# Adding products that nobody reads to TensorE beside the norms and the solver parts of a three-block diffusion transformer

## What is computed

```python
for l in range(3):
    h = norm(x) * (1 + sc_msa) + sh_msa
    q, k, v = split(h @ w_qkv + b_qkv)        # layer 1 also norms q and k per head
    o = softmax(q @ k.T / 3) @ v              # 16 heads, 512 x 512 scores each
    x = x + g_msa * (o @ w_proj + b_proj)
    h = norm(x) * (1 + sc_mlp) + sh_mlp
    x = x + g_mlp * mlp(h)                    # layer 0: top 2 of 4 experts
U, _ = qr(P)                                  # P is 144 x 64
R = expm(skew(silu(cond) @ W.T + b))          # 64 x 64, one per sequence
z = x @ U
return x + (z @ R - z) @ U.T
```

## Time and profile before

| | us |
|---|---|
| runs of the kernel | 918.87 median (909.43, 918.87, 920.58) |
| the profiled execution | 919.2 |
| its span, first to last instruction | 917.2 |
| PE busy | 751.5 (82% of the span) |
| DVE busy | 556.0 (61%) |
| ACT busy | 386.0 (42%) |
| POOL busy | 181.0 (20%) |
| mean granted clock of PE | 0.856 |

### The profile page before, as it was taken

The page is one execution under the profiler, slowest core; times in us unless marked ns, Lnnn a source line. Parts: engine busy times, 40 slices in busy tenths (PEclk is TensorE's granted clock), DMA queues, the critical chain, the costliest instruction groups (busy, mean ns, idle before and its releaser), DMA issues.

```text
span 917.2 us, 11092 instructions
## 1 busy us (share of the span) xinstructions
PE 751.5 (82%) x3571; PEld 438.5 (48%) x3571; DVE 556.0 (61%) x1614; ACT 386.0 (42%) x690; POOL 181.0 (20%) x372
## 2 busy tenths in 40 slices
PE   6597889967998799798867886979897789979746
PEld 1353444335764445366444343645443555436325
DVE  3477787886327558752465777474787666785242
ACT  0221465534444544254235442435453356646511
POOL 5502012440132300302323003021003110021020
PEclk9955899989997669799977997976897988999957
DMA  3210100110121000012100000100000101000000
GB/s 88 69 35 7 32 14 22 39 31 13 48 56 32 1 24 13 12 33 60 39 18 1 24 12 13 32 1 1 24 13 11 33 1 25 12 12 1 13 1 13
DMA packets 22714, 21.23 MB, mean 23 GB/s; under 512 B 4831, under 2 KB 17015, under 8 KB 22658
## 3 DMA queue, kind: packets, MB, share of 16 engines
q1 hardware_dynamic: 22610, 20.52, 8.6%
q10 hardware_dynamic: 48, 0.02, 0.0%
HBM read 13.62 MB, written 0.61 MB: 16 GB/s over the span
## 4 chain that ended last, share of the span: by engine, by line
PE 62%; DVE 28%; issue 4%; ACT 2%; POOL 2%; DMA 0%; DVEq 0%; SPq 0%; ACTq 0%; POOLq 0%
PE m_bank L1400 11%; PE o_bank L1422 10%; DVE row_max L972 9%; PE s_bank L1383 8%; PE d_bank L1539 7%; PE d_bank L1483 3%; PE m_bank L1592 3%; PE m_bank L1409 2%; DVE h_tok L1031 2%; PE d_bank L1528 2%; PE d_bank L1440 2%; PE d_bank L1439 1%; PE d_bank L1454 1%; PE d_bank L1530 1%; PE d_bank L1529 1%
## 5 line engine op out<-in xcount | busy, mean ns | idle before, releaser
L797 ACT ACTIVATE probs<-s_bank 128x512 f32<-128x512 f32 x384 | 223.1, 598 | 380.4 <-PE s_bank L1383 377.1
L972 DVE TENSOR_REDUCE row_max<-m_bank 128x1 fp32r<-128x512 f32 x384 | 255.3, 686 | 91.8 <-PE m_bank L1400 86.5
L1400 PE MATMUL m_bank<-k_pad,q_t 128*128 128x512 f32 x348 | 173.1, 511 | 43.0 <-DVE row_max L972 12.6
L1383 PE MATMUL s_bank<-q_t,k_pad 128*128 128x512 f32 x384 | 176.3, 466 | 2.9 <-ACT probs L797 2.0
L1400 PEld LDWEIGHTS m_bank<-k_pad,q_t 128*128 128x128 f32 x348 | 72.1, 212 | 115.0 <-issue 36.8
L1422 PE MATMUL o_bank<-probs,v_aug 128*32 128x512 f32 x768 | 120.6, 704 | 0.7 <-ACT probs L797 0.7
L1383 PEld LDWEIGHTS s_bank<-q_t,k_pad 128*128 128x128 f32 x384 | 81.8, 215 | 30.1 <-ACT probs L797 15.4
L1539 PE MATMUL d_bank<-w,g_act 128*128 128x144 f32 (+1 forms) x480 | 61.8, 288 | 8.7 <-issue 8.7
L1539 PEld LDWEIGHTS d_bank<-w,g_act 128*128 128x128 f32 (+1 forms) x480 | 59.5, 190 | 14.2 <-issue 8.3
L714 POOL TENSOR_TENSOR h_tok<-h_tok,mod 128x144 f32<-128x144 f32 x48 | 23.7, 494 | 202.7 <-DVE h_tok L1031 202.7
L1592 PE MATMUL m_bank<-gram_rows,ident 64*64 64x208 f32 (+42 forms) x128 | 40.3, 403 | 16.0 <-DVE gram_rows L1207 15.6
(11 more groups left out here) (232 smaller groups left out, 1145.1 us busy)
## 6 DMA issues: line engine op xcount, KB each, us to landing
k_pad<-k_t SPq DMA_DIRECT2D x96, 64.0 KB, 2.0
raw_a<-in_L_cond_w_dram SPq DMA_DIRECT2D x10, 288.0 KB
w<-in_L_cond_w_dram SPq DMA_DIRECT2D x10, 288.0 KB
w_rows<-in_L_cond_W_dram SPq DMA_DIRECT2D x8, 141.8 KB
raw_d<-in_L_cond_w_dram SPq DMA_DIRECT2D x30, 36.0 KB
x_tok<-in_x_dram SPq DMA_DIRECT2D x2, 288.0 KB, 4.5
w<-in_L_cond_W_fc_dram SPq DMA_DIRECT2D x2, 288.0 KB
raw_a<-in_L_cond_W_fc_dram SPq DMA_DIRECT2D x2, 288.0 KB
```

What stands on the lines that cost most here:

```text
L797: act.activation(probs[:, n % PROBS, :], s_banks[n % S_BANKS][:, :], ACT.Exp, scale=HD ** -0.5)\
L972: dve.tensor_reduce(row_max[:, grp % 2, t, MAXROW + 32 * j:MAXROW + 32 * j + 1], bk[:, :], AX.X, ALU.max).then_inc(drained, 1)
L1383: pe.matmul(s_banks[n % S_BANKS][:, :], k_pad[:, grp % PADS, j, kt * P:(kt + 1) * P], q_t[:, par, g, :], start=True, stop=True).then_inc(s ...
L1400: ins = pe.matmul(bk[:, :], q_t[:, par, g, t * P:(t + 1) * P], k_pad[:, grp % PADS, j, :], start=True, stop=True)
```

## The change

Three places issue products whose result nobody reads. Each is the 128x128 identity (fp32r) times itself repeated four times along the columns, so 128x512 with all rows and columns of the array in use.

1. **Solver parts.** From the start of the loop on (`busy_parts`), each solver part that uses a bank first issues one such product into its own bank: behind the wait for the bank, ahead of the wait for the part before it. 151 parts of the loop use a bank.
2. **Norms.** For the ten norms `(1, msa)` to `(4, mlp)` with a root, PE issues 12: four at once, three when DVE has added epsilon, three when the root is done, two when the third of the four `h_tok` tiles is written. DVE tells of the first two by a new semaphore `norm_part`, which takes the place of a wait on `dve_done` at the same two instructions. They go into the next free `d_bank`, and stand ahead of the `m_bank` that PE could take only once DVE is past the norm, or ahead of `max_turn` if that comes first.
3. **Roots of q and k.** For blocks 2 and 3, PE issues eight in the same manner: four, three when the last sum of squares is done, one when the root is done.

That makes 151 + 120 + 16 = 287 products. DVE, ACT, POOL and SP issue the same instructions in the same order as before.

```diff
--- before.py
+++ after.py
@@ -297,6 +297,10 @@
     def take(self):
         before, i = divmod(self.n, len(self.banks))
         self.n += 1
+        return self.banks[i], self.drained[i], before
+
+    def peek(self):
+        before, i = divmod(self.n, len(self.banks))
         return self.banks[i], self.drained[i], before
 
 
...
-        names = ("qk_copied qk_squared qk_scaled zeroed pads_zeroed ident_ready consts_ready weights_ready c_exp c_wide mods_part mods_full xn_ready "
+        names = ("qk_copied qk_squared qk_scaled zeroed pads_zeroed ident_ready consts_ready weights_ready c_exp c_wide mods_part mods_full norm_part xn_ready "
@@ -1017,8 +1021,11 @@
                             dve.bn_aggr(mean_var[:, i, :], stat[:, i, :]).then_inc(s["dve_done"], 1)
                         done[0] += T
                         dve.wait_ge(s["dve_done"], done[0])
-                        link(dve.tensor_scalar(nwt[:, 1, 0:T], mean_var[:, :, 1], EPS, None, ALU.add))
-                        rsqrt(rstd[:, :], nwt[:, 1, 0:T], nwt[:, 0, 0:T])
+                        dve.tensor_scalar(nwt[:, 1, 0:T], mean_var[:, :, 1], EPS, None, ALU.add)\
+                            .then_inc(s["norm_part"], 1)
+                        dve.wait_ge(s["norm_part"], seen.next("norm_part"))
+                        rsqrt(rstd[:, :], nwt[:, 1, 0:T], nwt[:, 0, 0:T], s["norm_part"])
+                        dve.wait_ge(s["norm_part"], seen.next("norm_part"))
                     if seen.n.get("norm", 0):
                         dve.wait_ge(s["h_turned"], T * seen.n["norm"])
                     else:
@@ -1351,8 +1358,29 @@
             stacks = {}
             h_ready = []
 
+            idle_at = []
+            busy_parts = [False]
+
+            def keep_busy(bk, count):
+
+                for _ in range(count):
+                    pe.matmul(bk[:, :], ident_r[:, :], ident_r[:, :].unsqueeze(1).to_broadcast([P, T, P]),
+                              start=True, stop=True)
+
+            def busy_beside_norm():
+
+                bk, drained, before = ring.peek()
+                n = idle_at.pop()[1]
+                pe.wait_ge(drained, before)
+                keep_busy(bk, 4)
+                for name, value, count in n:
+                    pe.wait_ge(s[name], value)
+                    keep_busy(bk, count)
+
             def take(r):
 
+                if r is mring and idle_at and mring.n >= idle_at[0][0]:
+                    busy_beside_norm()
                 bk, drained, before = r.take()
                 if before:
                     pe.wait_ge(drained, before)
@@ -1402,6 +1430,8 @@
                 ins.then_inc(s["max_full"], 1)
 
             def max_turn(grp):
+                if idle_at:
+                    busy_beside_norm()
                 for i in range(M_BANKS):
                     pe.wait_ge(m_drained[i], (mring.n + M_BANKS - 1 - i) // M_BANKS)
                 bk, placed[grp] = take(mring)
@@ -1442,6 +1472,11 @@
                 yield
 
             def norm(blk, kind):
+                if kind in ("msa", "mlp"):
+                    n = seen.next("norm_part")
+                    if (blk, kind) != (0, "msa") and (blk, kind) != (BLOCKS - 1, "mlp"):
+                        idle_at[:] = [(mring.n + M_BANKS + (not SOLVER_PLAN[FIRST_SLOT[("norm", blk, kind)]]),
+                                       (("norm_part", 2 * n - 1, 3), ("norm_part", 2 * n, 3), ("xn_ready", T * n - 1, 2)))]
                 yield
                 (a_bank, a_done), (d_bank, d_done) = take(ring), take(ring)
                 if not h_ready:
@@ -1474,6 +1509,9 @@
                                 pe.wait_ge(s["weights_ready"], LAYER_ITEM[l] + 1)
                             linear(bk[:, 0:3 * C], h_tile(t), lay_hi[:, l % 2, 0:3 * C], lay_lo[:, l % 2, 0:3 * C],
                                    lay_d[:, l % 2, 0:3 * C]).then_inc(s["qkv_full"], 1)
+                        if slot == 1 and l == 1:
+                            n = seen.next("root")
+                            idle_at[:] = [(mring.n + M_BANKS + 1, (("qk_squared", T * n, 3), ("qk_scaled", n, 1)))]
                     elif slot > 2:
                         (qb, q_done), (kb, k_done) = take(ring), take(ring)
                         seen.next("stack_ready")
@@ -1571,6 +1609,8 @@
                 if kind not in SOLVER_BANK:
                     return
                 bk, ready = take(mring)
+                if busy_parts[0]:
+                    keep_busy(bk, 1)
                 chain = 0 if step in QR_CHAIN else 1 if step in EXP_CHAIN else 2
                 if kind == "v_rows":
                     pe.wait_ge(s["v_summed"], VT)
@@ -1659,6 +1699,7 @@
                     solver(part)
             max_turn(0)
             woven = side(WOVEN)
+            busy_parts[0] = True
             for n in range(BLOCKS * STEPS):
                 grp = n // GSTEPS
                 if grp + 1 < BLOCKS * G:
```

## The result

| | before | after |
|---|---|---|
| median of the runs shown together (us) | 914.15 (908.42 to 920.58, 4 runs) | 928.23 (926.15 to 935.22, 4 runs) |
| the profiled execution, its span | 919.2, 917.2 | 928.67, 926.6 |
| mean granted clock | 0.856 | 0.911 |

The ratio is 1.0117, with a 95% interval of 1.0061 to 1.0173: the changed kernel is 0.6 to 1.7% slower. The forecast was 896, with a range up to 922. The clock did rise, and the time rose with it. Medians here are over all of a kernel's runs, while ratios leave out runs more than 1.5% above the fastest of the same kernel, so the two need not agree exactly.

The account below looks back on a forecast made before the run. PE was taken as the first bound, 62% of the chain and some 264 us at 1.2 GHz, with DVE close behind. 919.2 - 46.5 (clock) + 23.9 (added products) = 896.6, given as 896 us, range 872 to 922.

Parts of the forecast that it names:

- The clock's price: Loop stretches at the lower clock: each us there taken away saves 0.30 us, 61 us over all 24 stretches.
- the lower clock hardly matters: Rival for the whole kernel: only 9 us could be won from the clock, giving 934 us; chance 0.02.
- How much of it goes away: Loop's slow stretches: 117 us at norm and root gaps plus 38 elsewhere, together 155 us, worth 46.5.
- What the solver's products cost: Solver parts in the loop: 151 products at 0.23 us, 34.7 us of PE time, costing 21.5.
- The share that reaches the end: Solver parts: 0.62 of the products' added PE time was to lengthen the run, after PE's share of the chain.
- Bounds of 15 and 27: Solver parts: lower and upper limits in us for the products' cost, from shares of 0.45 and 0.77.
- What the groups cost: Norms and roots: 1.5 us for norm products that do not fit, 0.9 for a delayed turn, roots nothing.
- Roots: 0: Roots of q and k: eight products, 1.8 us, fit a gap of 4.30 us and cost 0.
- The turn at norm (3, mlp): Turn of the maxima at that norm: it waits for the third tile and two products, 0.9 us late.
- The clock stays low: Rival: the clock falls as often, with less than 80 us of slow time removed; 949 us, chance 0.10.
- The gain goes to DVE: Rival: the clock returns but DVE sets the pace, halving the rate to 0.15; some 910 us, chance 0.28.
- The signs: Loop: clock from 0.87 to about 0.97, PE busy 673.96 less 61 plus 287 products of about 0.4 us.

Follow-up runs that it names:

- e10: e5 with its added products on 32 rows and 32 columns of the array instead of 128 by 128; 925.07 us, ratio 1.0055 to the kernel before.
- e5: e1 with three groups moved one or two banks earlier and norm (3, mlp)'s last two products and their wait dropped; 902.45 us, ratio 0.9783 to before.
- e3: The changed kernel with all 287 products on 32 rows and 32 columns of the array instead of 128 by 128; 1007.38 us, ratio 1.0924 to before.
- e1: The changed kernel without the 151 solver-part products, keeping the 136 beside norms and roots; 915.66 us, ratio 0.9956 to before.
- e8: e5 plus products at only the 12 of 151 solver parts where a wait really follows; 901.45 us, ratio 0.9787 to before.
- e7: e2 with two products at each solver part instead of one; 960.6 us, ratio 1.0438 to before.
- e2: The changed kernel without the 136 products beside norms and roots, keeping the 151 at solver parts; 941.95 us, ratio 1.0243 to before.

## Why the prediction was wrong

**The clock's price: right.** "0.30 us for each us at the lower clock" measured 0.30 to 0.32 (e10 against e5) and 0.40 (e3 against after). A second reading agrees: for ten kernels (before, after, e1 to e8) I took the time of each of 23 groups of sixteen steps from the trace, and fitted it by what that group costs in every kernel, its us at the lower clock, and its added products. It gives 0.34 +- 0.01 us per us, 0.21 +- 0.01 for each of the 151 products (and of e7's 302), 1.0 +- 0.2 for a norm's or root's group as in after, and 0.7 +- 0.2 as in e5. The rival "the lower clock hardly matters" is excluded by e10. The Trainium skill ("TensorE: Matmul & The Clock Gate", section on HAM oscillation) would have it at 0.5; the runs stay below that.

**How much of it goes away: the first step that failed.** It said 85% of 137.6 us and 55% of 68.2, together 155; it was 103. Of the stretches with a norm's or root's gap some 53 us stayed, so 61% went. They are seven stretches; at two the group missed its gap (304.8, 738.4), at (4, msa) the clock was down from 601.8 on, ahead of the gap, one is the first, and three (461.8, 489.2, 567.7) stand close behind groups that had lain in their gaps. So filling a gap does not always hold the clock: e1's execution fell even at norm (0, mlp), behind the same twelve products:

```profile
200.00:206.80 6.80, 6.15 (x22) 3.34 (x23) 2.68 (x7) 1.20 (x2) 3.07 (x9) 0.50 0.00 0
```

Of those that follow no gap 48 us stayed, so 30% went, and one of 6.8 us (656.4) had PE busy throughout, with narrow solver products among the scores. Worth: 52 x 0.32 = 17 us.

**What the solver's products cost: the second.** "151 x 0.23 = 34.7 us of PE time" should have been 151 x 0.40 = 60. The share that reaches the end, 0.62, was near: measured 0.51 in after against e1, 0.63 in e2. So it was 31 us rather than 21.5. The row that would have told was in the trace of before: a solver row of 164 columns holds PE for 0.42 us, and its neighbours' loads don't overlap it; I took the distance from a place where they do. Bounds of 15 and 27 were too narrow for the same reason. Two readings behind them were wrong besides. The row with 16.0 us idle is the elimination's group alone; L1592 has a second one, for `lu`. And the chain's 3.4% belongs to both, so L1592's share of its own busy time is 31.2 / 60.5 = 0.52, where the prediction has 0.77:

```profile
L1592 PE MATMUL m_bank<-lu,ident 64*64 64x64 f32 (+42 forms) x128 | 20.2, 237 | 9.1 <-DVE lu L1243 9.1
```

That is close to the 0.51 measured, and would have spoken against the upper bound, not for it; it is the 0.23 that sank the term.

**What the groups cost: the third.** 2.4 us (1.5, and 0.9 for the turn) against 9. Most groups behaved as said: at norm (0, mlp) the twelve fit, PE resumes as soon behind the norm as before, nothing falls, and `pv` takes 1.07:

```profile
202.56 1.11 PE L1367 MATMUL d_bank<-ident_r 128*128 128x512 f32 x4
203.92 0.97 PE L1367 MATMUL d_bank<-ident_r 128*128 128x512 f32 x3 [0.25 <-DVE nwt L1024]
205.90 1.84 PE L1367 MATMUL d_bank<-ident_r 128*128 128x512 f32 x5 [1.01 <-DVE rstd L953]
208.61 0.51 PE L1367 MATMUL m_bank<-ident_r 128*128 128x512 f32 x1 [0.88 <-DVE gram_rows L1214]
...
209.89 1.07 PE L1452 MATMUL o_bank<-probs,v_aug 128*32 128x512 f32 x8
```

The three late ones were not foreseen: I read the gaps' lengths at four places and took the rest to be alike, and the shortest gap (3.12 us) told nothing of whether the group would stand in it. "Roots: 0" failed at block 2's. The turn at norm (3, mlp) was right in kind and near in size: DVE's norm ended at 705.96, and L983 started 0.65 us behind it, where it had started 0.08 ahead of the end (0.73 late, 0.9 forecast):

```profile
704.33 1.63 DVE L1038 TENSOR_SCALAR h_tok<-x_tok,mean_var,rstd 128x144 f32<-128x144 f32 x4
706.61 0.69 DVE L983 SCALAR_TENSOR_TENSOR q_t<-m_bank,q_t 128x512 fp32r<-128x512 f32 x1 [0.65 <-PE m_bank L1439]
```

**The sum, with what was measured:** 919.2 - 0.32 x 103 + 31 + 9 = 926, against 928.7 in the profiled execution. The forecast's two halves were 46.5 gained and 23.9 paid; it was 33 and 40.

**The rivals.** "The clock stays low" named its own turning point, less than 80 us taken away; 103 were, so it was not that. "The gain goes to DVE" would show as longer waits of the maxima for L976, but L1428 was idle for L976 for 5.3 us, where L1400 had waited 12.6 for L972, and DVE's share of the chain is 27% (28 before): not that. What happened was on none of the lists: a gain two thirds of the forecast, and a cost of 1.7 times it. **The signs:** the loop's clock was forecast at 0.97 and is 0.94; PE's busy time in the loop was forecast at 673.96 - 61 + 287 x 0.4 = 728 and is 720.62. That looks like a hit and is in part luck: at the prediction's own rate the clock saved only 81 x 103 / 205.8 = 41, so the products added some 87 and not 115. Their own rows come to 71.8 + 44.4 = 116, but these overlap the rows of their neighbours.

## What to carry to other kernels

Price an added matmul by the distance that it makes at the very place where it will stand, load included, not by the distance in a dense run of its own kind. If a product is to be free, it must stand ahead of the instruction at which the engine really comes to rest; find that instruction in the trace for each place, since a rule that counts banks misses some. And keep the two halves of such a change apart: filling real gaps paid 2% here once it was placed right, while filling busy time cost more than the clock gave back. And hold a trace's mean clock against the length of a product that you know: four of these thirteen lacked the record of their first low stretch.

## What the runs showed of the hardware that I had not expected

- 512 columns on 32x32 of the array keep PE busy as long as on 128x128 (477 and 475 ns), and the granted clock falls beside them as beside an idle PE: 352 us at the lower level in e3 against 155 in after.
- "Low" does not follow the times within one kernel, over e1's twelve runs from 186 to 225 us with no longer times, over e3's six from 289 to 394 at 0.13 us per us. A good part of that is no behaviour of the chip but the missing record above: e1's runs lie at 186 to 197 and at 208 to 225, and its trace has 34 us in the stretch that others lack. The 0.32 holds between kernels.
- The clock also falls behind stretches in which PE is busy nearly throughout (656.4 and 328.8 in after; before has falls at 653.5 and 329.3). Which part of the work there is too little for it was not tried alone.
